# Per-token attention: all 32 slices of products on VectorE, through two buffers, and none on GpSimd

## The reference

```python
q = (x @ Wq.T + bq).reshape(B, S, H, D)      # H = 32 heads, D = 16
k = (x @ Wk.T + bk).reshape(B, S, H, D)
v = (x @ Wv.T + bv).reshape(B, S, H, D)
scores = jnp.einsum('bshd,bsgd->bshg', q, k) * inv_sqrt_d
scores = jnp.where(scores > THRESH, scores, -jnp.inf)
attn = jax.nn.softmax(scores, axis=-1)
out = jnp.einsum('bshg,bsgd->bshd', attn, v).reshape(B, S, Hd)
return out @ Wo.T + bo
```

## Time and profile before

| | |
|---|---|
| Median of 3 runs | 1782.59 us (1775.65, 1782.59, 1785.02) |
| Profiled execution | 1777.76 us, its span 1776.0 us |
| VectorE busy | 1095.6 us (62%) |
| GpSimd busy | 287.1 us (16%) |
| TensorE busy | 1587.6 us (89%) |
| Mean granted clock of TensorE | 0.958 |

### The profile page before, as it was taken

One profiled execution on the slowest core, in us unless ns is written; L12 is line 12 of the kernel. 1 busy time (PEld: TensorE's weight loads), 2 busy tenths in 40 slices (PEclk: granted clock), 3 DMA queues, 4 the chain that ended last, 5 costly groups with the idle time before them and its releaser, 6 DMA issues. The chain is left out here.

```text
span 1776.0 us, 23311 instructions
## 1 busy us (share of the span) xinstructions
PE 1587.6 (89%) x7553; PEld 1201.8 (68%) x7553; DVE 1095.6 (62%) x2216; ACT 922.5 (52%) x1592; POOL 287.1 (16%) x248
## 2 busy tenths in 40 slices
PE   4999999999988557797899987968999999999996
PEld 4778788877863233485666656847777877877863
DVE  5665666666658962374588845736575576476473
ACT  4554554555445321263188864536565566556552
POOL 0000000000004410252266643510000000000000
PEclk9999999999999888899999998989999999999997
DMA  6011010101072006272432105540010100100011
GB/s 259 12 46 50 24 59 35 59 24 59 0 295 99 1 26 235 70 224 95 97 77 35 24 7 173 180 178 36 7 54 35 53 30 35 59 24 35 24 55 75
DMA packets 32555, 131.65 MB, mean 74 GB/s; under 512 B 5184, under 2 KB 7360, under 8 KB 23792
## 3 DMA queue, kind: packets, MB, share of 16 engines
q1 hardware_dynamic: 32496, 130.94, 22.3%
HBM read 125.16 MB, written 0.26 MB: 71 GB/s over the span
## 5 line engine op out<-in xcount | busy, mean ns | idle before, releaser
L1871 POOL TENSOR_TENSOR L2x_p_lo<-L2x_e_t,L2x_p_hi 128x512 fp32r<-128x512 f32 x80 | 105.3, 1326 | 63.0 <-ACT L2x_p_hi L2056 62.3
L746 DVE TENSOR_TENSOR L0x_k_lo<-bank,L0x_k_hi 128x512 fp32r<-128x512 f32 x128 | 85.8, 689 | 42.4 <-ACT L0x_k_hi L635 42.0
L746 DVE TENSOR_TENSOR L3x_k_lo<-bank,L3x_k_hi 128x512 fp32r<-128x512 f32 x128 | 85.4, 688 | 39.8 <-ACT L3x_k_hi L635 39.8
L389 PE MATMUL bank<-L0x_ctx_hi,L0x_w_hi 128*128 128x512 f32 x256 | 103.6, 405 | 4.2 <-DVE L0x_ctx_lo L661 4.2
L389 PE MATMUL bank<-L3x_ctx_hi,L3x_w_hi 128*128 128x512 f32 x256 | 102.7, 401 | 4.3 <-DVE L3x_ctx_lo L661 4.2
L635 ACT ACTIVATE L0x_k_hi<-bank 128x512 fp32r<-128x512 f32 x128 | 74.2, 599 | 54.6 <-PE bank L511 54.6
L635 ACT ACTIVATE L3x_k_hi<-bank 128x512 fp32r<-128x512 f32 x128 | 73.9, 599 | 53.2 <-PE bank L511 53.2
L390 PE MATMUL bank<-L3x_ctx_lo,L3x_w_hi 128*128 128x512 f32 x256 | 101.0, 395 | 0.0
L391 PE MATMUL bank<-L0x_ctx_hi,L0x_w_lo 128*128 128x512 f32 x256 | 101.0, 394 | 0.0
L391 PE MATMUL bank<-L3x_ctx_hi,L3x_w_lo 128*128 128x512 f32 x256 | 101.0, 394 | 0.0
L390 PE MATMUL bank<-L0x_ctx_lo,L0x_w_hi 128*128 128x512 f32 x256 | 100.0, 390 | 0.0
(11 more groups left out here) (630 smaller groups left out, 4407.0 us busy)
## 6 DMA issues: line engine op xcount, KB each, us to landing
L0x_w_kqv<-in_L0x_kqv SPq DMA_DIRECT2D x7, 1536.0 KB, 6.3
L3x_w_kqv<-in_L3x_kqv SPq DMA_DIRECT2D x7, 1536.0 KB, 6.2
L0x_w_o<-in_L0x_o SPq DMA_DIRECT2D x8, 1024.0 KB, 4.8
L1a_w_o<-in_L1a_o SPq DMA_DIRECT2D x8, 1024.0 KB, 7.1
L2a_w_o<-in_L2a_o SPq DMA_DIRECT2D x8, 1024.0 KB, 7.4
L3x_w_o<-in_L3x_o SPq DMA_DIRECT2D x8, 1024.0 KB, 4.8
L0x_s<-in_ctx_t SPq DMA_DIRECT2D x4, 1024.0 KB, 13.3
L0a_w<-in_L0a_w SPq DMA_DIRECT2D x4, 1024.0 KB, 10.9
```

What stands on the lines that cost most here:

```text
L389: pe.matmul(out, left[0], right[0], start=start, stop=False)
L746: dve.tensor_tensor(p_lo[:, kt % 4, :], ring_bank(kt)[:], bits(p_hi[:, kt % 4, :]), ALU.subtract).then_inc(p_ready, 1)
L1871: pool.tensor_tensor(p_lo[:, t % 8, :], e_of(t), bits(p_hi[:, t % 8, :]), ALU.subtract).then_inc(low_pool, 1)
```

## The change

All 32 products are made by VectorE, alternately into the two halves of `prod`. GpSimd's loop, its two buffers and its semaphore are gone; GpSimd keeps the clearing of old semaphores. Before product `n` VectorE waits for reduction `n - 2`, whose buffer it writes.

```diff
-        prod = st.sb("prod", [P, HP * H * E])
-        prod_pool = st.sb("prod_pool", [P, 2, HP * H * E])
+        prod = st.sb("prod", [P, 2, HP * H * E])
...
-                for phase in range(2):
-                    if phase == 0:
-                        pool.wait_ge(qkv_biased, 3)
-                    else:
-                        pool.wait_ge(kept, 1)
-                    for i in range(1, PARTS, 2):
-                        n = phase * PARTS + i
-                        if n >= 5:
-                            pool.wait_ge(summed, n - 3)
-                        shape, left, right = factors(phase, i)
-                        view = prod_pool[:, (n // 2) % 2, :].rearrange("p (a b c) -> p a b c", a=shape[1], b=shape[2])
-                        pool.tensor_tensor(view, left, right, ALU.mult).then_inc(pool_ready, 1)
...
                     for i in range(PARTS):
                         n = phase * PARTS + i
                         shape, left, right = factors(phase, i)
-                        split = dict(a=shape[1], b=shape[2])
-                        if i % 2 == 0:
-                            if n >= 2:
-                                dve.wait_ge(summed, n - 1)
-                            view = prod[:].rearrange("p (a b c) -> p a b c", **split)
-                            dve.tensor_tensor(view, left, right, ALU.mult).then_inc(prod_ready, 1)
-                            prods += 1
-                            dve.wait_ge(prod_ready, prods)
-                        else:
-                            view = prod_pool[:, (n // 2) % 2, :].rearrange("p (a b c) -> p a b c", **split)
-                            dve.wait_ge(pool_ready, n // 2 + 1)
+                        view = prod[:, i % 2, :].rearrange("p (a b c) -> p a b c", a=shape[1], b=shape[2])
+                        if n >= 2:
+                            dve.wait_ge(summed, n - 1)
+                        dve.tensor_tensor(view, left, right, ALU.mult).then_inc(prod_ready, 1)
+                        dve.wait_ge(prod_ready, n + 1)
                         dve.tensor_reduce(dst[:, i * HP:(i + 1) * HP, :], view, AX.X, ALU.add).then_inc(summed, 1)
                         if i % 2 and tile <= KT:
                             keys.vector(dve, tile)
```

More of the change, by code:

```diff
@@ L974, in per_token_head_attention @@
         prod_ready = st.sem("prod_ready")
-        pool_ready = st.sem("pool_ready")
         summed = st.sem("summed")
@@ L1064, in _ @@
                 dve.wait_ge(qkv_biased, 3)
-                prods, tile = 0, 0
+                tile = 0
                 def sum_parts(phase, dst):
-                    nonlocal prods, tile
+                    nonlocal tile
                     for i in range(PARTS):
```

## The result

The change makes the kernel slower by 0.36% in the first measurement: 1786.99 us against 1779.95 us, medians of 20 runs each, ratio 1.0036 with an interval from 1.0024 to 1.0048, +6.4 us. The profiled execution took 1785.95 us, its span is 1784.2 us.

The account below looks back on a forecast made before the run. VectorE was taken to bound the stage; +0.5 us in the first phase and +1.8 in the second made +2.3, from the 1782.59 us median to 1784.9 us. The range was 1777 to 1790 us.

Parts of the forecast that it names:

- What bounds the stage: Both product phases: VectorE sets the stage's time, busy 42.22 of 43.60 us and 52.65 of 53.00 us.
- its products stood still for GpSimd: Both phases: VectorE's product waits while GpSimd works, ending 1.09 us (first) or 1.69 us (second) behind GpSimd's end.
- The sum: Both phases: +0.5 us in the first and +1.8 us in the second, together +2.3 us.
- one lone product: Second phase: its product running without GpSimd, seen once at 1.87 us, taken for all sixteen products.
- the lower bound from the tails (1.69): Second phase: sixteen products at 1.69 us would make 27.0 us, and the whole sum -0.6 us.
- The second buffer: Products on VectorE: lets each overlap the last 0.08 us of the reduction ahead, 1.3 us over 16.
- Cover: First phase's tightest place: key projection ready 2.3 us before VectorE takes it; 1.4 us would stay.
- the rival that TensorE becomes the bound: First phase: a clock staying low makes TensorE slower than VectorE's pairs, +18 us, 1803 us; chance 0.06.
- Products at one rate: Second phase: products take 1.20 us like the first's, whatever the strides; sum -8.4 us, 1774.2 us; chance 0.04.
- the tail moves with it as a whole: Behind the stage: the tail starts from VectorE's last key instruction (645.2 us) and shifts unchanged with it.
- the likeliest case: Whole kernel: the forecast with chance 0.72, 1782.0 to 1785.6 us by its costs.
- a later clock: Output projection and next stage: TensorE's clock rises after both (+1.3, +2.0 us) or before (-2.3, -1.6); 1781 to 1788.2 us; chance 0.18.

Follow-up runs that it names:

- GpSimd beside the sums: Kernel before, but GpSimd starts each product once VectorE's product of the pair before is complete, and VectorE makes slice 1 of each phase; ratio 0.9897, repeated 0.9913.
- the experiment on v: Changed kernel with v read as if the heads were innermost and adjacent, stride one element instead of 16, computing another result; ratio 0.9937 against the kernel before.
- the four late reductions: Kernel before with four more VectorE reductions, results unused, in the last pair of the second phase; ratio 1.0047.
- the second phase alone: Kernel before with VectorE making all products of the second phase only, GpSimd still helping in the first; ratio 1.0013.
- the repeated change: The changed kernel measured again beside the experiments, against the kernel before; 12 runs, ratio 1.0022, +3.9 us.

## Why the prediction was right, and where it was off

**What bounds the stage.** VectorE, as said: in the two phases it had one wait of 1.0 us before and has none after, and the phases grew by what its row of instructions grew. That its products stood still for GpSimd is confirmed from both sides: without GpSimd all take 1.21 and 1.88 us, and with GpSimd beside reductions all but the first ones beside it take 1.20 to 1.23 and 1.86 to 1.91 us. The rule of the Trainium skill on the ports (SBUF — State Buffer) agrees in its other half as well: a reduction has one input in SBUF and is not held up, 1.22 us beside GpSimd.

**The sum.** Forecast for the two phases +0.5 and +1.8 us, measured +0.73 and +2.01. The products were 1.212 and 1.878 us, not 1.20 and 1.87, and the reductions behind VectorE's own products take 1.220 us where those on GpSimd's took 1.210. The value read off one lone product held; the lower bound from the tails (1.69) was rightly not taken. The second buffer was forecast at 1.3 us and is worth 2.1, since a product that must wait for the reduction ahead starts later than its end.

**Cover.** It was forecast to shrink from 2.3 to 1.4 us at the place that the prediction takes. It did not: the projection there now runs from 565.09 us for 5.17, and VectorE takes the tile at 572.64, 2.4 us behind its end. The transposes ahead of it, which wait for ScalarE's copy of an earlier tile, start earlier too, and both took less time, 0.79 and 5.17 us in place of 1.09 and 5.50. VectorE never waited for a projection, so the rival that TensorE becomes the bound is refuted for the change. Pairs of 4.23 us, with GpSimd beside the sums, are where the cover ends: there VectorE waited for projections, 0.16 to 0.40 us at a time.

**Products at one rate.** Refuted for the stride that the kernel has, and right for adjacent elements. The rule of the Trainium skill (VectorE: DVE Perf Modes) gives an estimate of 1.22 us; the experiment on v measured 1.213 us, and the change 1.878 with the stride. The formula has no term for a stride, and "whatever its strides" in the prediction is a reading of it; the measurement decides against that reading.

**The step that was off: "the tail moves with it as a whole", and the clock behind it.** The forecast of the likeliest case ended with the stage: +2.3 us. Measured were +6.4 and +3.9 us. The tail did keep its length (15.80 and 15.89 us). But the stages behind did not. I had priced a later clock at up to +3.3 us, as a rival, for two projections; the output projection moved by 0.1 us, and the trace shows +2.3 us in the next stage, +1.0 in the one behind it and +3.0 in the last cross attention. That these lengths are not set by the program is shown, since the same program gave 14.85 and 12.52 us; that they go with the clock is read from the stretches, 0.50 against 0.82 in the next stage and 0.91 against 1.00 in the cross attention.

Whether the change makes the long case more likely is not settled. For it: the first measurement's lower limit of +4.3 us, above the +2.8 of the phases; its mean clock of 0.955; and the four late reductions, +5.9 at the least for 5.0, with a clock lower by 0.005. Against it: the second phase alone, with the same last pair, at +2.3 us (-0.5 to 5.0), the repeated change, whose clock was lower by less than 0.001 and which stands +3.1 us above at equal clock, and the long stages in traces without the change. A sum that ends at the stage was good to 0.5 us; as a forecast of the whole it was too small by 1.6 to 4.1 us.

**Where luck helped.** The time of 1786.99 us lies in the stated range, 1777 to 1790, but above the 1782.0 to 1785.6 of the likeliest case and within the 1781 to 1788.2 of the rival on the clock, which had a chance of 0.18. It would have been further off from the right starting point: the median of three runs, 1782.59 us, was 2.6 us above that of twenty, 1779.95, and this made up for more than half of the 4.1 us that the sum lacked.

## What to carry to other kernels

When VectorE multiplies two operands from SBUF while GpSimd does the same, look at when VectorE's instruction ends against GpSimd's end. If it always ends nearly one own duration behind (1.09 us for a product of 1.20 here, 1.69 for 1.87), GpSimd's help is not parallel, and what it saves is what VectorE does with one operand meanwhile. Then don't take the work away from GpSimd: start it behind VectorE's product, so that it runs beside reductions; that was worth 15 to 18 microseconds here, and moving all to VectorE cost three in the stage. Before a surplus behind the change is explained, profile the same program twice and compare the stages, and keep the granted clocks of all runs, of both kernels.

## What the runs showed of the hardware that was not expected

The feed-forward stage behind, in which TensorE works with gaps, does not have one length: it took 14.9 us in the first trace of the change and 12.5 in the second, with the same instructions, and the last cross attention 540.7 and 538.0. A product with one operand read at a stride of 16 fp32 elements costs 0.67 us more per 1024 elements, 0.65 ns for each. A product that starts behind one of GpSimd ends a fixed time behind GpSimd's end, 1.07 to 1.09 us in the first phase, where it started 0.4 to 1.8 us before that end, and 1.67 to 1.71 in the second, where it started 0.8 to 2.3 us before. And TensorE's idle time is paid for later: six unused projections in a gap of 6.2 us shortened the tail behind them by 3.4 to 3.7 us, at a clock of 0.96 to 1.00 in place of 0.50 to 0.55.
